# A factorisation tower on one core: row numbers in 22 operations, gathers laid out anew, a chunk's passes and x1 two banks later

## The reference, cut to what matters

```python
for W in [f0, f1, f2]:                       # xk starts as x0 = e
    z = einsum('bfd,bgd->bfgd', x0, xk).reshape(b, f * g, d)
    xk = einsum('bpd,pm->bmd', z, W)         # 128 maps per layer
result = sum(concat(outs, axis=1), axis=-1)  # 512 x 384
h = relu(concat([result, dense_ctx]) @ W_top1 + b_top1)   # 400 -> 512
h = relu(h @ W_top2 + b_top2)                             # 512 -> 256
y = h @ W_top3
```

## Time and profile before

| | |
|---|---|
| median of 3 runs | 701.36 us |
| the profiled execution's own time | 699.4 us |
| its span | 697.3 us |
| TensorE busy | 641.7 us (92%), granted clock 0.998 |
| VectorE busy | 572.9 us (82%) |
| ScalarE busy | 383.4 us (55%) |
| GpSimd busy | 531.2 us (76%) |
| DMA | 41.91 MB, 60 GB/s over the span |

### The profile page before, as it was taken

How to read it: one execution, slowest core, us unless ns; L and a number is a source line. 1 busy time by engine, 2 the same in 40 slices (tenths; PEclk the granted TensorE clock), 3 DMA queues, 4 the chain that set the end, 5 groups by cost and what they waited for, 6 DMA issues and landing times.

```text
span 697.3 us, 11588 instructions
## 1 busy us (share of the span) xinstructions
PE 641.7 (92%) x2942; PEld 508.3 (73%) x2942; DVE 572.9 (82%) x2038; ACT 383.4 (55%) x1157; POOL 531.2 (76%) x528
## 2 busy tenths in 40 slices
PE   3068789899999999999999999999999999999998
PEld 1046567677777788887877788887877888887877
DVE  6096779798989798898969798898969898898870
ACT  0426457475747465655647465565657475655531
POOL 6613999889899989897978989897977989575420
PEclk9999999999999999999999999999999999999999
DMA  9637230221213040303022040403022040300000
GB/s 175 90 105 266 54 111 11 60 61 48 73 40 83 6 116 6 113 10 111 10 63 57 6 116 6 113 11 111 9 67 53 10 112 5 111 0 2 1 0 1
DMA packets 70580, 41.91 MB, mean 60 GB/s; under 512 B 45745, under 2 KB 55361, under 8 KB 70386
## 3 DMA queue, kind: packets, MB, share of 16 engines
q1 hardware_dynamic: 57886, 35.51, 18.8%
q10 hardware_dynamic: 7380, 4.38, 3.4%
q0 software_dynamic: 5248, 1.29, 1.9%
HBM read 39.18 MB, written 1.94 MB: 59 GB/s over the span
## 4 chain that ended last, share of the span: by engine, by line
PE 69%; DVE 10%; issue 8%; POOL 8%; ACT 2%; DMA 1%; ACTq 0%; POOLq 0%; DVEq 0%
PE y L848 17%; PE y L850 16%; PE y L849 16%; DVE scaled L750 6%; PE side L855 4%; PE late L866 4%; PE acc L830 3%; PE acc L825 3%; PE acc L824 2%; POOL z_parts L455 2%; POOL emb_quads L444 2%; ACT scaled L552 2%; POOL sum L470 1%; PE y L866 1%; PE late L877 1%
## 5 line engine op out<-in xcount | busy, mean ns | idle before, releaser
L750 DVE SCALAR_TENSOR_TENSOR scaled<-y,x_rows,scaled 128x128 f32<-128x128 f32 x1728 | 466.1, 341 | 79.5 <-ACT scaled L552 50.0
L552 ACT ACTIVATE scaled<-y,x_rows 128x128 f32<-128x128 f32 x768 | 218.3, 366 | 226.3 <-PE y L850 214.8
L848 PE MATMUL y<-w_hi,x_parts 128*128 128x512 f32 (+1 forms) x640 | 277.3, 433 | 5.7 <-DVE x_parts L717 2.7
L850 PE MATMUL y<-w_hi,x_parts 128*128 128x512 f32 (+1 forms) x640 | 248.7, 389 | 0.0
L849 PE MATMUL y<-w_lo,x_parts 128*128 128x512 f32 (+1 forms) x640 | 248.6, 388 | 0.0
L455 POOL TENSOR_TENSOR z_parts<-z,z_parts 117x512 fp32r<-117x512 f32 (+1 forms) x107 | 138.8, 1297 | 47.4 <-ACT z_parts L506 46.3
L444 POOL DMA_INDIRECT emb_quads<-in_small_tables_dram,quad_rows x144 | 136.5, 948 | 25.8 <-issue 13.2
L848 PEld LDWEIGHTS y<-w_hi,x_parts 128*128 128x128 f32 x640 | 120.6, 188 | 42.6 <-DVE scaled L750 16.9
L850 PEld LDWEIGHTS y<-w_hi,x_parts 128*128 128x128 f32 x640 | 120.0, 187 | 26.0
L849 PEld LDWEIGHTS y<-w_lo,x_parts 128*128 128x128 f32 x640 | 121.0, 189 | 18.7
L470 POOL TENSOR_TENSOR sum<-sum,scaled 128x512 f32<-128x512 f32 x63 | 81.8, 1298 | 32.3 <-DVE scaled L750 31.5
(11 more groups left out here) (95 smaller groups left out, 364.0 us busy)
## 6 DMA issues: line engine op xcount, KB each, us to landing
z<-x_turned SPq DMA_DIRECT2D x311, 78.0 KB
x_three<-x_turned SPq DMA_DIRECT2D x48, 78.0 KB
x_turned<-emb_quads SPq DMA_DIRECT2D x156, 8.0 KB
w_sb<-in_w_dram SPq DMA_DIRECT2D x1, 2496.0 KB
emb_quads<-in_small_tables_dram,quad_rows POOLq DMA_INDIRECT x144
s_sb<-in_w_dram ACTq DMA_DIRECT2D x12, 160.0 KB
x_turned<-emb_singles SPq DMA_DIRECT2D x89, 2.0 KB
x_stack<-x_turned SPq DMA_DIRECT2D x48, 19.5 KB
```

Source lines behind the costliest of these rows:

```text
L552: done = act.activation(scaled[:, k % 2, BY_ACT.index(j), i * M:(i + 1) * M], y2[n % RING][:, i * M:(i + 1) * M], ACT.Copy, scale=x0_rows[ ...
L750: dve.scalar_tensor_tensor(part, y2[n % RING][:, i * M:(i + 1) * M], x0_f, part, ALU.mult, ALU.add).then_inc(terms_in, 1)
L848: pe.matmul(dst, x1_hi[:, t % 2, cols], hi, start=True, stop=False)
L850: pe.matmul(dst, x1_lo[:, t % 2, cols], hi, start=False, stop=True).then_inc(y_ready, 1)
```

## The change

QUADS becomes the packed fields in order, four at a time: the last set has two fields. That gives 23 stores a tile where there were 22. All the lists over quads (gathers, stores on SP and on ScalarE's queue) run in QUAD_ORDER, the sets with several stores first. Row numbers are made in 6 operations over all 128 partitions and all groups (`small_numbers`: table number times 12500 plus id, the table numbers read by a broadcast DMA of `row_numbers`) and 16 copies that move them to the quads' partitions (`quad_numbers`), all at the start; they wait for all ids. Of tile 2's 10 gathers eight come in slots 0 to 7 of tile 0, the others in slots 14 and 20. The singles of a group are spread over the tiles ahead of it. CONTRACT_LAG is 10 and X1_AT 36, except that tile 1's chunks keep lag 8. In tile 0 the three_blocks come behind the turned rows.

```diff
@@ -35,13 +35,17 @@
 CHUNKS = 12500
-QUADS = ((0, 1, 2, 3), (5, 6, 7, 8), (9, 10, 11, 12), (13, 14, 15, 16), (17, 18, 19, 36),
-         (21, 22, 23, 24), (25, 26, 27, 28), (29, 30, 38), (32, 33, 34))
 SINGLES = (4, 20, 31, 35, 37)
+PACKED = tuple(f for f in range(39) if f not in SINGLES)
+QUADS = tuple(PACKED[i:i + 4] for i in range(0, SMALL, 4))
+
+QUAD_ORDER = (8, 4, 7, 0, 1, 2, 3, 5, 6)
 TURNED = 20
 GATHER_AHEAD = 14
+
+THIRD_TILE_AT = (0, 1, 2, 3, 4, 5, 6, 7, 14, 20)
@@ -74,8 +78,9 @@
 LOW_LAG = 3
-CONTRACT_LAG = 8
-X1_AT = 34
+CONTRACT_LAG = 10
+FIRST_CONTRACT_LAG = 8
+X1_AT = 36
 FIRST_X1_AT = 36
@@ -108,16 +113,9 @@
     return [(i, f, n, (f, F + f) if f < TURNED else (f,)) for i, f, n in found]
-def alike(j):
-
-    found = []
-    for i, fields in enumerate(QUADS):
-        if j < len(fields):
-            if found and found[-1][1] == i and fields[j] == found[-1][2] + 4 * (i - found[-1][0]):
-                found[-1][1] += 1
-            else:
-                found.append([i, i + 1, fields[j]])
-    return found
+def neighbours():
+
+    return [(i, i + n, f) for i, f, n, _ in runs(PACKED)]
@@ -182,24 +180,33 @@
     return [f for f in range(F) if tables[f].shape[0] <= CHUNKS * ROWS]
+def singles_of(u):
+
+    if u < TPG:
+        return [(1, i) for i in {2: (0,), 3: (1, 2)}[u]]
+    found = [(1, i) for i in (3, 4)] if u == TPG else []
+    g, q = (u + TPG - 1) // TPG, (u + TPG - 1) % TPG
+    return found + [(g, i) for i in ((0,), (1,), (2, 3), (4,))[q] if 1 < g < GROUPS]
+
+
 def gathers_of(u):
-    g, q = u // TPG + 1, u % TPG
-    cuts = (0, 0, 0, 3, len(SINGLES))
-    singles = [(True, g, i) for i in range(cuts[q], cuts[q + 1])] if g < GROUPS else []
-    return singles + [(False, u, i) for i in range(len(QUADS))]
+    singles = [(True, g, i) for g, i in singles_of(u)]
+    own = [x for x in singles if x[1] == u // TPG]
+    return own + [(False, u, i) for i in QUAD_ORDER] + [x for x in singles if x not in own]
 def gathers_at(t, s):
+    if t == 0 and s in THIRD_TILE_AT:
+        return [x for x, at in zip(gathers_of(2), THIRD_TILE_AT) if at == s]
     found = []
-    for u in range(max(2, t + 1), min(t + 4, TILES)):
-        first = max(0, (u - 2) * SLOTS - GATHER_AHEAD)
-        last = (u - 1) * SLOTS - GATHER_AHEAD
+    for u in range(max(3, t + 1), min(t + 4, TILES)):
+        first = (u - 2) * SLOTS - GATHER_AHEAD
         x = t * SLOTS + s - first
-        if 0 <= x < last - first:
+        if 0 <= x < SLOTS:
             items = gathers_of(u)
-            found += items[len(items) * x // (last - first):len(items) * (x + 1) // (last - first)]
+            found += items[len(items) * x // SLOTS:len(items) * (x + 1) // SLOTS]
     return found
@@ -376,7 +384,7 @@
                     store_singles(sp, u, copies)
-                for i in range(len(QUADS)):
+                for i in QUAD_ORDER:
                     store_quad(sp, u, i, copies)
@@ -394,6 +402,7 @@
             sp.dma_start(ids_sb[:, 0, :], ids[0:P, :]).then_inc(ids_in, 16)
+            sp.dma_start(table_number[:, 0, :], row_numbers[0:1, 0:SMALL].to_broadcast([P, SMALL])).then_inc(numbers_in, 16)
             sp.dma_start(ids_sb[:, 1:GROUPS, :], ids[P:B, :].rearrange("(g p) f -> p g f", p=P)).then_inc(rest_ids_in, 16)
@@ -407,8 +416,10 @@
                     turned_rows(sp, u, c)
-                    if c == 2:
+                    if c == 2 and u > 0:
                         three_blocks(u)
+                if u == 0:
+                    three_blocks(u)
                 if u == 1:
@@ -435,11 +446,9 @@
                 n = len(QUADS[i])
-                if i == 0 and u < TPG:
-                    pool.wait_ge(quads_first, u + 1)
-                if i == 0 and u == TPG:
-                    pool.wait_ge(quads_rest, TPG)
-                if u >= 2 and i == 0:
+                if i == QUAD_ORDER[0] and u < TPG:
+                    pool.wait_ge(quads_ready, u + 1)
+                if i == QUAD_ORDER[0] and u >= 2:
                     pool.wait_ge(stored[u % 2], 16 * STORES * (u // 2))
@@ -612,10 +621,10 @@
             store_singles(act, 0, (1,))
-            for i in range(len(QUADS)):
+            for i in QUAD_ORDER:
                 if any(len(rows) > 1 for _, _, _, rows in runs(QUADS[i])):
                     store_quad(act, 0, i, (1,))
-                if i == 1:
+                if i == 0:
                     store_singles(act, 1, (0, 1))
@@ -677,22 +686,20 @@
         def _(dve):
-            def quad_numbers(groups, q):
+            def small_numbers():
+
+                for a, b, f in neighbours():
+                    done = dve.scalar_tensor_tensor(
+                        small_rows[:, :, a:b], table_number[:, :, a:b].to_broadcast([P, GROUPS, b - a]), CHUNKS * ROWS,
+                        ids_sb[:, :, f:f + b - a], ALU.mult, ALU.add)
+                return done
+
+            def quad_numbers(q):
                 for j in range(FPB):
-                    for a, b, f in alike(j):
-                        done = dve.tensor_tensor(
-                            quad_rows[SPT * j:SPT * j + SPT, groups, q, a:b],
-                            ids_sb[SPT * q:SPT * q + SPT, groups, f:f + 4 * (b - a - 1) + 1:4],
-                            table_at[SPT * q:SPT * q + SPT, j:j + 1, a:b].to_broadcast(
-                                [SPT, groups.stop - groups.start, b - a]), ALU.add)
-                return done
-
-            def tables_begin_at():
-
-                for i, fields in enumerate(QUADS):
-                    for j, f in enumerate(fields):
-                        done = dve.memset(table_at[:, j, i:i + 1], small.index(f) * CHUNKS * ROWS)
+                    n = len(range(j, SMALL, FPB))
+                    done = dve.tensor_copy(quad_rows[SPT * j:SPT * j + SPT, :, q, 0:n],
+                                           small_rows[SPT * q:SPT * q + SPT, :, j:SMALL:FPB])
                 return done
@@ -767,19 +774,18 @@
             dve.memset(x0_rows[:, :, :, F:FS], 1.0).then_inc(blank, 1)
-            tables_begin_at().then_inc(tables_begin, 1)
-            dve.wait_ge(tables_begin, 1)
             dve.wait_ge(ids_in, 16)
+            dve.wait_ge(rest_ids_in, 16)
+            dve.wait_ge(numbers_in, 16)
+            small_numbers().then_inc(small_in, 1)
+            dve.wait_ge(small_in, 1)
             for q in range(TPG):
-                quad_numbers(slice(0, 1), q).then_inc(quads_first, 1)
+                quad_numbers(q).then_inc(quads_ready, 1)
             dve.wait_ge(weights_in, 48)
             dve.memset(diag[:, :, :, :, :], 0.0).then_inc(no_diag, 1)
-            dve.wait_ge(rest_ids_in, 16)
-            for q in range(TPG):
-                quad_numbers(slice(1, GROUPS), q).then_inc(quads_rest, 1)
             dve.wait_ge(w0_hi_in, 1)
@@ -958,7 +964,7 @@
                     layer2(t * SLOTS + s)
-                    c = chunk_at(t + 1, s, CONTRACT_LAG)
+                    c = chunk_at(t + 1, s, CONTRACT_LAG if t > 0 else FIRST_CONTRACT_LAG)
                     if c is not None:
...
```

More of the change, by code:

```diff
@@ L231, in cross_network @@
         quad_rows = sb("quad_rows", [P, GROUPS, TPG, len(QUADS)], I32)
-        table_at = sb("table_at", [P, FPB, len(QUADS)])
+        small_rows = sb("small_rows", [P, GROUPS, SMALL], I32)
+        table_number = sb("table_number", [P, 1, SMALL])
         emb_quads = sb("emb_quads", [P, 2, len(QUADS), D])
@@ L280, in cross_network @@
         rest_ids_in = sem("rest_ids_in")
-        quads_first = sem("quads_first")
-        quads_rest = sem("quads_rest")
+        numbers_in = sem("numbers_in")
+        small_in = sem("small_in")
+        quads_ready = sem("quads_ready")
         weights_in = sem("weights_in")
@@ L293, in cross_network @@
         no_diag = sem("no_diag")
-        tables_begin = sem("tables_begin")
         w0_sum = sem("w0_sum")
```

## The result

On one chip the kernel before took 702.9 us (median of 5) and the changed one 694.63 us (median of 5, 690.99 to 697.67): a ratio of 0.9889, 95% interval 0.9847 to 0.9931. Forecast were 692.3. The gain is small, 1.1%, but clear of 1. The profiled execution is the quickest, 690.99 us with a span of 689.0; against 699.4 of before that is 8.4 less, as between the medians (8.3). One execution each of e5, of e7's second run and of before on chip E was slow (763.94, 811.64 and 911.85 us, at a granted clock of 0.832, 0.761 and 0.665); the ratios leave them out.

The account below looks back on a forecast made before the run. TensorE was taken as the bound from tile 5 on, with waits on VectorE (head) and GpSimd (tile 0) before. 699.4 - 10.4 - 5.8 - 6.1 + 13.2 = 690.3, plus 1.96 for the median: 692.3 us, range 688 to 696.

Parts of the forecast that it names:

- Head, -10.4: Before TensorE's first bank: without the second lot of row numbers on VectorE the first product comes earlier, gaining 10.4 us.
- rival C: Head: SP takes VectorE's place as the limit, gain there only 5 to 7 us, total 696 to 698; chance 0.16.
- Rival D: Head: VectorE's stall belongs to the profiled execution, so the head gives nothing; 702.7 us, 1.3 slower; chance 0.13.
- Tile 0, -5.8: Tile 0: gathers moved earlier free GpSimd and remove TensorE's three waits for low parts; gain 5.8 us, bounds 4 and 6.
- rival E: Tile 0: the eight gathers reach beyond low part (1,0), delaying it; about 697 us; chance with others 0.07.
- Lag, -6.1: Contract two slots later from tile 2's chunks on removes TensorE's waits for GpSimd's low parts; gain 6.1 us, bounds 4 and 7.
- x1, +13.2: Tile starts: x1 two slots later makes TensorE's bank 0 wait for x1_low; costs 13.2 us, bounds 5 and 19.
- Rival B: Tile starts: the later x1 costs little, its gap before bank 0 hidden in others; 679 to 686 us; chance 0.14.
- the 0.58 for the five tiles that begin with a wait: Later x1 at tiles 2, 3, 4, 8 and 12, already waiting for VectorE: 0.58 us each, 2.9 in all.
- TensorE has no idle time behind it in these tiles to win that back: Later x1 at the nine other tiles from 5 on: each 1.15 us delay of bank 0 stays, 10.3 in all.

Follow-up runs that it names:

- e5: The kernel before with X1_AT 36 instead of 34 alone, on chip C: 713.11 us, ratio 1.0154 to the kernel before.
- e7: Changed kernel plus 56 small VectorE additions in the second lot of row numbers' old place, run twice: 692.99 us (1.0027, chip D), 693.04 us (1.0028, chip E).
- second pair: Kernel before and changed kernel, both unchanged, profiled again on chip C: 701.41 and 694.8 us, ratio 0.9912.
- e3: Changed kernel with X1_AT 34, lag 8 and the old gather schedule, so only the head is changed, on chip B: 690.72 us, ratio 0.9985.
- b2: The kernel before, unchanged, profiled on chip D, where it took 690.9 us; profiled span 690.4 us.
- e1: Changed kernel with X1_AT back at 34, lag 10 kept, on chip B: 675.28 us, ratio 0.9759 to the kernel before.
- a1: The changed kernel, unchanged, run again on chip C beside the kernel before: 694.8 us, ratio 0.9912.
- e6: The kernel before with contract lag 10 from tile 2's chunks on, alone, on chip C: 695.37 us, ratio 0.9919.
- e2: Changed kernel with X1_AT 34 and contract lag back at 8, on chip B: 679.86 us, ratio 0.9838 to the kernel before.
- b1: The kernel before, unchanged, profiled again on chip C: 701.41 us.
- e9: Changed kernel with X1_AT 34 and FIRST_X1_AT 35, all else as changed, on chip D: 673.39 us, ratio 0.9752 to the kernel before.

## Why the prediction was right, and where it was not

**The total** was right, 694.63 for 692.3, for a chip like that of the profile. It hangs on one term, the head's gain, and that gain is the stall's: that the result was measured on a chip that has the stall is luck. On chips D and E, by e7, there is no gain.

**Head, -10.4.** As forecast: w1_lo ends at 30.50 (30.5), first product 33.27 (31 to 36), first bank 45.95 (44 to 49), GpSimd unharmed by the added wait. SP was mostly freed (0.88 us a store, 1.3 before), hence -11.5, nearer the upper bound than I took. In the second pair SP was not (1.2 us a store), the turned rows land late, and the gain is 56.39 - 49.60 = 6.8: rival C's mechanism and figure. On chips B, D and E it is nothing (e3's ratio on B, b2 and e7 on D, e7's ratio on E). Rival D was right in its consequence: it forecast 1.3 us more than before, and e7 shows 0.3% more. Its cause, the recording alone, is not shown: b2 is recorded in the same way and has no gap. The rule cited beside it (the Trainium skill, "NOTIFIC — the notification-queue block", sections 7.1 and 7.2) says that the block holds a producer back rather than lose a record, and those sections give no load at which it does. b2 shows that recording these 56 operations is not enough for the gaps; whether the block has a part in them where they occur, no run here shows. The argument against D, that unrecorded runs would be shorter than the profiled one, decided nothing: every timed run here lists a granted clock, and a run without a record wasn't tried.

**Tile 0, -5.8.** Measured -4.8, or 36.20 us without the stall (forecast 36 to 37). No wait for a low part is left in it, and rival E is out: GpSimd ends its eighth gather at 51.34 and then idles 3.97 us (forecast: 4.0 left over). Between 36.2 and the 37.59 of after lies a pause of ScalarE, here in order of time in after, then in e1:

```profile
51.24 0.43 ACT L531 ACTIVATE diag<-x_rows,mask_sb 32x160 f32<-32x160 f32 x1
52.90 1.14 ACT L561 ACTIVATE scaled<-y,x_rows 128x128 f32<-128x128 f32 x4 [1.23 <-PE y L856]
```
```profile
51.18 0.43 ACT L531 ACTIVATE diag<-x_rows,mask_sb 32x160 f32<-32x160 f32 x1
51.64 1.14 ACT L561 ACTIVATE scaled<-y,x_rows 128x128 f32<-128x128 f32 x4
```

TensorE then stands 0.39 and 0.53 us at banks 8 and 9; banks 7, 8 and 9 start 1.25 and 1.49 us apart, in e1 0.69 each. a1 shows it too (1.60 and 1.03). It costs 1.4 us. It stands only in the two profiles of the changed kernel on chips A and C, and in none of the kernel before, so that it is a late part of the stall is a guess and not shown.

**Lag, -6.1.** Alone on before it is -7.3 (e6), with the gathers spread -4.5 (e2 to e1), and the spreading itself brings -2.3 in tiles 1 to 15 (e3 to e2). The forecast's -6.1 held both, since it counted the gathers that leave tiles 4 and 8; measured -6.8. The spreading takes 1.8 each out of those two tiles and puts 1.2 into tile 2.

**x1, +13.2: the term that was mis-sized.** The mechanism is right, and so is the sign named for it: tiles 5, 6, 9, 10, 13 and 14 are each 1.1 to 1.2 us longer than before. Rival B (it costs little) is out. But I priced it beside the wrong neighbours. Alone it is +11.3 (e5), with lag 10 +15.45, so 4.1 us come from the pair of edits. The step that was mis-sized is the 0.58 for the five tiles that begin with a wait. From bank 36 to bank 4 of the next tile, after against e1, tiles 2, 3, 4, 8 and 12 lose 0.84 to 1.20 us each (5.5 together, 2.9 forecast), the nine others 10.4 (10.3 forecast). At lag 8 (e5 against before) the five lose 0.57 each, just as forecast, and the nine 8.1. At lag 8 bank 0 of tiles 2 to 4, 8 and 12 is followed by a wait of 0.5 us for VectorE (bank 1 comes 1.33 us after it), which a late bank 0 swallows: in e5 the distance is 0.78, and tile 4 grows by 0.2 only. With lag 10 that wait is nearly gone before x1 moves (0.72 in e1), nothing swallows the gap, and tile 4 grows by 0.7. In tile 5 it is the distance from bank 1 to bank 2 (1.01 at lag 8, 0.83 at lag 10): the tile grows by 1.0 and by 1.4. "TensorE has no idle time behind it in these tiles to win that back" was wrong for the kernel before by 0.1 to 0.2 a tile, right for the changed one.

The errors cancel: head -1.1, tile 0 +1.0, lag and spreading -0.7, x1 +2.2; tiles 1 to 15 of before on chip A and of e3 on chip B differ by 0.7 more.

## What to carry to other kernels

A stall of an engine behind which nothing is named should be seen in a second execution on another chip before it is put into a sum: here it was worth 7 to 11.5 us on two chips (or one, run twice) and nothing on three. Price an edit beside its companions: when one edit removes waits, the next one's gap loses its cover. And an operand at a tile's border belongs as early as its inputs allow; two banks later cost 11 to 15 us of 700. Look at what else a constant moves: with x1 one bank later the operand was still in time, and the sum beside it cost 7 us.

## What the runs showed of the hardware

On chips A and C VectorE is held up between some 15 and 36 us, and in most executions SP is too. It stands in all four profiles taken there of kernels with the old row numbers; here e6 on chip C, VectorE:

```profile
28.74 0.32 DVE L685 TENSOR_TENSOR quad_rows<-ids_sb,table_at 32x3 int32<-32x3 int32 x3 [5.17 <-issue]
32.31 0.32 DVE L685 TENSOR_TENSOR quad_rows<-ids_sb,table_at 32x3 int32<-32x3 int32 x3 [3.25 <-issue]
35.88 2.31 DVE L685 TENSOR_TENSOR quad_rows<-ids_sb,table_at 32x3 int32<-32x3 int32 x22 [3.25 <-issue]
```

In a1, where VectorE has no small operations in the stretch, SP's stores still take 1.2 us each against 0.89 in b2: the old operations didn't cause SP's delay. That they were only many enough to suffer is likely, but no run put other small operations there on such a chip. It differs from run to run (SP 0.88 us a store in after, 1.2 in a1) and is absent in all profiles from chips B, D and E. Loading of code is not behind it: the trace of before has DMA packets of instructions at 6.7 and 50.1 us and none between. What it is, and why it ends at 36 us, stays open.

TensorE's granted clock falls from 2.4 to 1.2 GHz for one or a few stretches of about 3.4 us per execution. One costs some 1.5 us: behind the last bank the rest of the span takes 22.3 us with none (before), 23.9 with one (b1, e9) and 25.2 where it is twice as long (b2, e1). Ahead of a1's first bank, at the end of a head in which TensorE had little to do, the granted clock is 0.56 of full speed on average (the third number from the end; the columns are the stretch, its length, busy us of PE, PEld, DVE, ACT and POOL, PEclk, DMA share, GB/s):

```profile
35.00:40.00 5.00, 2.06 (x4) 1.24 (x5) 1.74 (x3) 1.07 (x2) 0.00 (x0) 0.56 0.65 201
```
